# A state-space convolution with a routed low-rank layer on one core: odd x blocks turned by VectorE, outer-product tables made four heads at a time

## The reference, cut to what matters

```python
u_m = u * mask                                  # mask: position < length of the row
K[h, l] = 2 Re sum_n Cs[h, n] exp(dtA[h, n] l)  # 64 modes, 1024 taps
y = (causal convolution of u_m with K) + u_m * D ; y = y * mask
logits = y @ route_w.T                          # 8 experts
gate = one_hot(argmax) * max(logits)
out = x + sum_e gate[e] * (y @ A[e].T) @ Bw[e].T
```

## Time and profile before

| | us |
|---|---|
| three runs | 623.93, 623.76, 622.61; median 623.76 |
| the profiled execution, and its span | 623.93, 622.1 |
| PE, PEld (weight loads), DVE busy | 591.5, 530.9, 542.5 |
| ACT, POOL busy | 379.3, 372.9 |
| load of x, 512 KB, x64, median to landing | 4.1 |
| store, 512 KB, x63 | 4.8 |
| skewed load (Traw), 128 KB, x64 | 2.9 |

### The profile page before, as it was taken

How to read it: one execution, slowest core, us unless ns; L and a number is a source line. 1 busy time by engine, 2 the same in 40 slices (tenths; PEclk the granted TensorE clock), 3 DMA queues, 4 the chain that set the end, 5 groups by cost and what they waited for, 6 DMA issues and landing times.

```text
span 622.1 us, 13886 instructions
## 1 busy us (share of the span) xinstructions
PE 591.5 (95%) x3681; PEld 530.9 (85%) x3681; DVE 542.5 (87%) x1436; ACT 379.3 (61%) x1164; POOL 372.9 (60%) x474
## 2 busy tenths in 40 slices
PE   3379999999999999999999999999999999999995
PEld 2268998999899889988998998899899989988984
DVE  7778889988988898899889888988998898889874
ACT  3676656766676666567666766665676667666520
POOL 4465566557656755675576567556755765676520
PEclk9989999999999999999999999999999999999998
DMA  6023534453454345435534543454345345434521
GB/s 137 17 56 108 152 110 128 147 150 96 142 149 132 113 139 153 112 126 146 152 96 139 151 133 110 141 152 114 125 146 152 98 136 151 139 105 140 154 78 67
DMA packets 37074, 77.68 MB, mean 125 GB/s; under 512 B 11836, under 2 KB 20350, under 8 KB 36998
## 3 DMA queue, kind: packets, MB, share of 16 engines
q1 hardware_dynamic: 27846, 43.76, 29.5%
q10 hardware_dynamic: 9152, 33.03, 13.0%
HBM read 43.16 MB, written 33.62 MB: 123 GB/s over the span
## 4 chain that ended last, share of the span: by engine, by line
PE 92%; DVE 4%; issue 2%; POOL 1%; ACT 0%; DMA 0%; POOLq 0%
PE psYo L987 19%; PE psZ L1009 19%; PE psO L987 15%; PE psYe L987 12%; PE psS L987 11%; PE psO L1036 5%; PE psXe L1000 4%; PE psXo L1000 4%; PE psZ L1078 1%; PE psS L1047 1%; DMA logs<-in_L_cond_log_dt_dram 0%; DVE ex L693 0%; POOL Grev L436 0%; POOL wave L426 0%; DVE fraction L803 0%
## 5 line engine op out<-in xcount | busy, mean ns | idle before, releaser
L468 POOL TENSOR_TENSOR Slo<-Sf,Shi 128x384 fp32r<-128x384 f32 x64 | 64.9, 1015 | 210.1 <-ACT Shi L590 210.1
L852 DVE SCALAR_TENSOR_TENSOR brought<-Sf,tab,psS 64x128 f32<-64x128 f32 x256 | 89.0, 348 | 47.3 <-ACT Sf L585 40.9
L1009 PE MATMUL psZ<-Wt,Y 128*128 128x136 f32 x1024 | 129.6, 280 | 0.0
L1009 PEld LDWEIGHTS psZ<-Wt,Y 128*128 128x128 f32 x1024 | 127.8, 191 | 0.1
L531 ACT ACTIVATE Ghi<-Grev 128x256 fp32r<-128x256 f32 x64 | 26.8, 418 | 94.2 <-POOL Grev L436 94.2
L884 DVE TENSOR_TENSOR ost<-psO,xt 128x512 f32<-128x512 f32 x128 | 82.0, 676 | 2.2 <-PE psO L987 2.2
L461 POOL TENSOR_TENSOR Xlo<-xeven,Xhi 128x512 fp32r<-128x512 f32 x64 | 82.8, 1293 | 0.0
L568 ACT ACTIVATE Xhi<-psXe 128x512 fp32r<-128x512 f32 x64 | 38.2, 597 | 38.3 <-PE psXe L1000 38.3
L789 DVE TENSOR_SCALAR whole<-turns_t 128x256 f32<-128x256 f32 x64 | 57.8, 903 | 4.1 <-ACT turns_t L519 4.1
L585 ACT ACTIVATE Sf<-psS 128x128 f32<-128x128 f32 x64 | 17.7, 277 | 66.4 <-PE psS L987 66.4
L987 PE MATMUL psYo<-Xhi,Thi 128*128 128x512 f32 x128 | 55.6, 434 | 0.0
(11 more groups left out here) (194 smaller groups left out, 1670.8 us busy)
## 6 DMA issues: line engine op xcount, KB each, us to landing
xt<-in_x_dram SPq DMA_DIRECT2D x64, 512.0 KB, 4.1
out_dram<-ost ACTq DMA_DIRECT2D x63, 512.0 KB, 4.8
Traw<-kdram SPq DMA_DIRECT2D x64, 128.0 KB, 2.9
kdram<-krow SPq DMA_DIRECT2D x64, 1.0 KB
A_nat<-in_L_ffn_A_dram SPq DMA_DIRECT2D x1, 512.0 KB, 4.9
B_nat<-in_L_ffn_Bw_dram SPq DMA_DIRECT2D x8, 64.0 KB, 3.6
out_dram<-ost SPq DMA_DIRECT2D x2, 256.0 KB, 2.0
lens_i<-in_itok_B_dram SPq DMA_DIRECT2D x1, 64.0 KB, 3.6
```

The costliest lines, as they stand in the source:

```text
L468: pool.tensor_tensor(Slo[h.s2][:, :], Sf[h.s2][:, :], Shi[h.s2][:, :].bitcast(F32), ALU.subtract).then_inc(slo_done, 1)
L852: dve.scalar_tensor_tensor(brought[to, :], Sf[h.s2][fr, old], tab2[fr, BR, h.n:h.n + 1], psS[to, new], ALU.mult, ALU.add).then_inc(brought ...
L1009: last = pe.matmul(psZ[:, 0:NW], Y[:, j, c, :], Wt[:, 2 * c + j, :], start=(j == 0 and c == 0), stop=(j == 1 and c == NE - 1), skip_group_ ...
```

## The change

1. Odd x blocks. `turn_x` turns only the even blocks on PE. The odd ones are loaded a second time from DRAM, in 16 DMAs a head (32 rows by 4 groups by 32 positions, 128 bytes each), laid out so that a DVE transpose in 32x32 squares gives the position-major tile `xodd`. SP issues 11 of the 16, ACT 5. ACT rounds from `xodd`; the odd remainder goes to POOL (`x_lo_odd`).
2. `carry` writes what it brought into psS in place of the tile `brought`; the experts' `rank` is in psZ.
3. Tables. In place of 256 angles a head: 16 coarse and 16 fine ones, for four heads at once (`Part`), sines and magnitudes on those, and an outer product per head: real and imaginary halves (`mirror` makes the second set), a 512-wide product `both` and a sum of its halves.
4. The order in each engine's step, the start (steps for head 0 are written out, `run_steps` begins at 1) and the place of the exponentials of heads 8 to 63 (ACT, step 2) are different. The weight copies of the start go from DVE to ACT; the skewed load is issued at the start of SP's next step.

```diff
+        def load_blocks(eng, h, pieces):
+            need(eng, xodd_done, h.n - 1)
+            for g, c in pieces:
+                eng.dma_start(xblk[h.s2][g * G32:(g + 1) * G32, c, :, :],
+                              bass.AP(x.tensor, h.n * L + c * Q + P + g * G32,
+                                      [[H * L, G32], [G32 * H * L, G4], [1, G32]])
+                              ).then_inc(blk_in[h.s2], 16)
...
             def step(head):                                     # SP
+                if head(1).there and not is_head(head(0), 1):
+                    skew_kernel(head(1))
                 if head(2).there:
+                    load_blocks(sp, head(2), PIECES[:11])
                     load_x(head(2))
                     write_kernel(head(2))
-                    skew_kernel(head(2))
...
+            def weigh(part):                                    # POOL
+                for table, half, size in ((coarse, 0, COARSE), (fine, 0, FINE), (fine, 1, FINE)):
+                    pool.tensor_tensor(table[:, half, part.heads, :], wave[:, size, 0:part.n, :],
+                                       mag[:, size, part.heads, :], ALU.mult).then_inc(weighed, 1)
             def g_table(h):
+                pool.tensor_tensor(both[:, :, :, :],
+                    coarse[:, :, h.n, :].rearrange("p t (a b) -> p t a b", b=1).to_broadcast(wide),
+                    fine[:, :, h.n, :].rearrange("p t (a b) -> p t a b", a=1).to_broadcast(wide),
+                    ALU.mult).then_inc(both_done, 1)
+                pool.tensor_tensor(Grev[h.s2][:, :], both[:, 0, :, :].rearrange("p a b -> p (a b)"),
+                                   both[:, 1, :, :].rearrange("p a b -> p (a b)"), ALU.add).then_inc(grev_done, 1)
+            def x_lo_odd(h):
+                need(pool, xhi_odd, h.n + 1)
+                pool.tensor_tensor(Xlo[h.s2][:, 1, :], xodd[:, :], Xhi[h.s2][:, 1, :].bitcast(F32),
+                                   ALU.subtract).then_inc(xlo_odd, 1)
             def step(head):                                     # POOL
+                if part_at(head(8)): angle_steps(part_at(head(8)))
+                if part_at(head(6)): turn_parts(part_at(head(6)))
+                if part_at(head(4)): weigh(part_at(head(4)))
+                g_table(head(3)); x_lo_odd(head(1)); s_lo(head(0)); x_lo(head(1)); t_lo(head(1)); g_lo(head(3))
...
             def step(head):                                     # ACT
+                load_blocks(act, head(2), PIECES[11:])
+                store(head(-2)); first_state(head(0)); x_hi_odd(head(1)); m_matrix(head(3))
+                x_hi_even(head(1)); b_hi(head(2)); s_hi(head(0)); x_even(head(1)); t_hi(head(1)); g_hi(head(3))
+                if part_at(head(7)): turns(part_at(head(7)))    # four of 64 elements
+                if part_at(head(4)): mirror(part_at(head(4)))   # four half-height copies
+                w_hi(head(-1)); k_row(head(2))
+                if is_head(head(0), 2): magnitudes(slice(2 * FIRST, H))
+                if part_at(head(5)): sines(part_at(head(5)))
...
+            def turn_blocks(h):                                 # DVE
+                need(dve, blk_in[h.s2], (h.half + 1) * 16 * G4 * NE)
+                need(dve, xlo_odd, h.n)
+                dve.transpose(xodd[:, :], xblk[h.s2][:, :, :, :].rearrange("p c g i -> p (c g i)")
+                              ).then_inc(xodd_done, 1)
...
-                        dve.scalar_tensor_tensor(brought[to, :], Sf[h.s2][fr, old],
+                        dve.scalar_tensor_tensor(psS[to, new], Sf[h.s2][fr, old],
...
             def step(head):                                     # DVE
+                turn_blocks(head(1)); carry(head(0)); largest(head(-1)); first_largest(head(-1))
+                first_best(head(-1)); gates(head(-1)); gated(head(-1)); b_lo(head(2)); w_lo(head(-1))
+                cut(head(0), 0); cut(head(0), 1); add(head(-1), 0); add(head(-1), 1)
+                if part_at(head(7)): whole_turns(part_at(head(7)))
+                if part_at(head(6)): fractions(part_at(head(6))); clamp(part_at(head(6)))
...
             def step(head):                                     # PE
+                bring(head(0)); turn_x(head(1)); inputs(head(2)); project(head(-1)); within(head(0), 0)
+                within(head(0), 1); turn_k(head(2)); turn_wh(head(-1)); from_states(head(0)); up(head(-1), head(2))
```

More of the change, by code:

```diff
@@ L262, in __init__, with part_at @@
                 self.there = 0 <= n < H
+        class Part:
+            def __init__(self, k, start, stop):
+                self.k = k
+                self.start = start
+                self.n = stop - start
+                self.heads = slice(start, stop)
+        EDGES = list(range(0, H + 1, FIRST))
+        parts = [Part(k, EDGES[k], EDGES[k + 1]) for k in range(len(EDGES) - 1)]
+        def part_at(h):
+            for part in parts[2:]:
+                if part.start == h.n:
+                    return part
+            return None
         def is_head(h, *numbers):
@@ L409, in _, with angle_steps @@
             pool.wait_ge(tab_done, 1)
[L410 to L420, removed]
+            def angle_steps(part):
+                need(pool, turns_done, part.k * 4)
+                need(pool, frac2_done, part.k * 2)
+                for t, table in ((step_h, VH), (step_t, V), (step_l, VL)):
+                    pool.tensor_tensor(t[:, 0:part.n, :],
+                                       tab1[:, table, part.heads].rearrange("p (h a) -> p h a", a=1)
+                                       .to_broadcast([P, part.n, G16]),
+                                       grid16[:, :].rearrange("p (a g) -> p a g", a=1)
+                                       .to_broadcast([P, part.n, G16]), ALU.mult).then_inc(steps_done, 1)
@@ L471, in step @@
             def step(head):
-                if head(0).there and not is_head(head(0), 0):
+                if part_at(head(8)):
+                    angle_steps(part_at(head(8)))
+                if part_at(head(6)):
+                    turn_parts(part_at(head(6)))
+                if part_at(head(4)):
+                    weigh(part_at(head(4)))
+                if head(3).there and not is_head(head(0), 1):
+                    g_table(head(3))
+                if head(1).there:
+                    x_lo_odd(head(1))
+                if head(0).there:
                     s_lo(head(0))
@@ L475, in step @@
                     x_lo(head(1))
-                if head(3).there:
+                if head(3).there and is_head(head(0), 1):
                     g_table(head(3))
@@ new lines, in mirror @@
+            def mirror(part):
+                need(act, weighed, part.k * 3 + 3)
+                top, low = slice(0, N), slice(N, P)
+                for table, to, half, fr, scale in ((coarse, low, 1, top, 1.0), (coarse, top, 1, low, -1.0),
+                                                   (fine, low, 0, top, 1.0), (fine, top, 1, low, 1.0)):
+                    act.activation(table[to, half, part.heads, :], table[fr, half if table is fine else 0, part.heads, :],
+                                   ACT.Copy, scale=scale).then_inc(mirrored, 1)
@@ L904, in step @@
                     gated(head(-1))
-                if head(1).there and not is_head(head(0), 0):
-                    x_lo(head(1))
                 if head(2).there:
@@ L1123, in turn_tables @@
                 last.then_inc(tabs_turned, 1)
-            first = [Head(n) for n in range(2)]
-            pe.wait_ge(consts, 10)
-            turn_x(first[0], 0)
-            turn_x(first[0], 1)
+            first = [Head(n) for n in range(3)]
+            pe.wait_ge(consts, 9)
+            turn_x(first[0])
             pe.wait_ge(pack1_done, 1)
@@ L1153, in _ @@
                     last.then_inc(b_turned, 1)
+            inputs(first[0])
+            turn_k(first[0])
+            bring(first[0])
+            turn_x(first[1])
             inputs(first[1])
             turn_k(first[1])
-            pe.wait_ge(w_done, 3)
+            within(first[0], 0)
+            within(first[0], 1)
+            inputs(first[2])
+            from_states(first[0])
+            turn_k(first[2])
             run_steps(step)
```

448 lines of the change are left out of this document (246 added, 202 removed).

## The result

The changed kernel takes 679.7 us (median of 4 runs, 678.21 to 685.37) against 623.18 us before (4 runs, 622.46 to 623.93): a ratio of 1.0919, interval 1.0869 to 1.097. It is 9% slower; the forecast was 604.5 us, 590 to 627. The profiled execution of the changed kernel took 680.76 us.

A forecast was written before the change was run, and what follows sets the result against it. The prediction took PE to bound the kernel from the third step on; 623.93 us, less 26.4 for PE, plus 12 for the shared port, less 5 for the start, gave 604.5 us, range 590 to 627.

The forecast's parts named there:

- Issue: SP's queue: each small load holds it 0.32 us plus a 0.05 gap, a round of 6.0 of 8.56 us, no bound.
- The landing: SP's queue: from the k row's write to the skewed load, taken as 1.17 us of the round.
- Rival (d): SP and ACT queues: small loads at 0.6 us each hold SP 9.1 us a step; 625 us, chance 0.08.
- The pieces: DMA engines: 2048 pieces of 128 bytes a head at 15 ns, 1.9 us a step, hidden.
- (c): DMA engines become the bound: at 45 ns a piece 9.8 us a step, 667 us; chance 0.10.
- PE: Steady steps: four transposes a head go, 0.44 us, so the step falls from 9.00 to 8.56 us, -26.4 us in all.
- The cover: Steady step: the POOL state remainder ends 0.31 us before PE wants it, the slack read as next to run out.
- The transpose: DVE: the new 128x512 SBUF to SBUF transpose takes 0.65 us, between 0.64 and 1.3.
- (b): DVE: the transpose takes 1.3 us, waits for POOL and delays the carry; 634.5 us, chance 0.11.
- The shared port: DVE and POOL: a part's angle ops wait for POOL, 0.8 us for each of 15 parts, +12 us.
- The price of zero for the PSUM operands: DVE: the PSUM destinations of carry and rank cost nothing, within 0.05 us an op either way.
- The start: First steps: an earlier first `bring`, smaller angle sets and moved exponentials and weight copies gain 5 us.

The follow-up runs named there:

- e_xfirst: The changed kernel with the x load issued ahead of SP's eleven small loads instead of behind them: 625.18 us, 1.0042 of the kernel before.
- e_four_big: The changed kernel with each head's 2048 pieces, from other addresses of x, in four DMAs, two each on SP and ACT: 607.7 us.
- e_no_loads: The changed kernel without the small loads of heads 3 to 63, VectorE turning old data: 608.11 us, 0.9761 of the kernel before.
- e_ceiling: The kernel before the change with three of the four odd transposes of each head left out: 621.19 us, 0.9962 of the kernel before.
- e_quad: The changed kernel, complete, with the odd blocks of four heads in 16 DMAs of 512 pieces, four issued a step: 606.8 us.
- e_small: The changed kernel with its 16 small loads a head cut to 32 pieces each in place of 128: 662.92 us.
- e_inter: The changed kernel with SP's order changed to five small loads, skewed load, x load, six small loads, k row's write: 629.55 us.
- e_quad_sbuf: e_quad with the intermediate results of the carry and the ranks back in SBUF: 667.02 us, 1.0694 of the kernel before.

## Why the prediction was wrong, point by point

**Issue: the step that failed.** The prediction had SP's round at 1.17 + 13 x 0.37 = 6.0 us and "no bound under 0.57 us a piece". Both terms were too small. The 0.37 came from a 128-piece skewed load of the earlier trace rows; a small load takes about 0.5 and, over 62 rounds, 0.54: the mean step of 10.01 less 0.25 for the write, 2.67 for the wait behind it (165.3 / 62), 0.23 for ACT (14.5 / 62) and 0.93 for skew, x load and gaps leaves 5.9 us for eleven. The landing was the second term, read as a constant. It was 1.17 us in a kernel whose write went out long after the x load; now the write follows the 512 KB x load by 0.5 us, and write to skew is 2.9 us, 0.25 + 2.67. By these means neither error alone would have bound: 2.9 + 13 x 0.37 = 7.7 and 1.17 + 13 x 0.54 = 8.2 are both under 8.8; together they make 9.9. And 0.54 is still under the 0.57 that the prediction allowed for: what broke that margin is the landing. That the issue time alone would have been free is not shown, though: in e_xfirst, with a landing of 1.73 us on average, the round is 9.08 us and still binds. And the x load at the end of the round, said to have "most of a step" left, has none once the round is the step; e_xfirst, which moves only it, brings back 54.5 us, with its effect on the landing in them.

**Rival (d)** named the right mechanism and the right sign in the trace (SP without waits for ACT), but with the landing at 1.17 it came to 625 us, and it had a chance of 0.08.

**The pieces.** Right: hidden. e_four_big costs no time against e_no_loads, which rules out (c). The DMA share rises by 0.14 of a step of 8.81 us: 1.2 us, or 9.6 ns a piece, by an estimate, where I took 15. The Trainium skill, "DMA: Bandwidth & Descriptors", section "Specifications", asks for at least 512 B a transfer for line rate. No run here tests that rule: at 128 B and a share of 0.63 the engines are not full, and the time shows nothing of it.

**PE.** The 0.44 us are gone and a step of 8.56 us exists, but one in four. The cover that I read from the earlier trace rows, 0.31 us, was not the nearest: in e_ceiling, PE with 0.33 us less waits for DVE's `wh` after 0.04 us. That the saving comes through because the change moves `turn_wh` back too, which my sum put at nothing, is argued and not shown.

**The transpose.** 0.70 us for 0.65, and never long beside POOL, so (b) is out.

**The shared port.** Forecast 0.8 us a part; four steps of e_no_loads sum to 35.30 us, 1.06 over 4 x 8.56. The ops named are the ones lengthened (0.89 and 0.23 us in e_quad, up to 0.64 for the clamp beside `Grev` at 61.71 us of the changed kernel). Why the second and third step of four are long too (8.87, 8.69) was not followed op by op. The price of zero for the PSUM operands was right only as the difference to before; without them e_quad loses 60 us.

**The start.** Forecast -5. The second `bring` comes 5.7 us earlier (37.25 for 42.98 in e_no_loads), but the next step takes 13.7 us for 10.5, and at the fourth `bring` 2.6 us are left (59.93 for 62.52). The end, which I didn't price, gained 1.2: 18.6 us from the last `bring` to the end in e_no_loads for 19.7 (17.8 in the changed kernel).

**The account.** 679.7 - 604.5 = 75.2 us: the loads' issues, the landing and their clock 71.6, and by e_no_loads the start +2.4, the step +2.7 (60 x 0.045, 8.805 for the forecast mean of 8.76) and the end -1.2, which is 0.3 too much. Without the failed step the forecast would have been 3.6 us low; that this part came out so close is partly luck, since it priced the long steps at one in four and the second and third of four are long as well.

## What to carry to other kernels

Count a queue's round in DMAs, not in bytes, and add to it every wait that stands in it. A landing time read from the old trace holds only for the old order: ask what big load goes out just ahead. Where a saving needs many small loads, give each one as many pieces as its pattern can hold; and test how much the bounding engine can give back before the next one takes over.

## What the runs showed of the hardware

- The issue of a small load takes some 0.5 us of SP's queue with 32 pieces (eleven in 5.06 to 7.26 us, e_small) and with 128 (5.17 to 7.25, the changed kernel), and 0.48 with 512 in most steps, up to 1.2 in the others (e_quad). Right behind a 512 KB load it takes 0.62 on average, ahead of it 0.48 (e_inter); on ACT 0.44 (changed kernel). The skewed load takes 0.34 and the 1 KB write 0.25.
- 2048 pieces of 128 bytes a step, from rows 256 KB apart, cost no visible time at a DMA share of 0.63 (e_four_big).
- From the issue of a 1 KB write to that of the load that waits for its landing it is 1.2 us where the queue was idle before (the kernel before), 3.0 on average some 0.5 us behind a 512 KB load on the same queue (the changed kernel), and 1.73 behind eleven small loads with the 512 KB load ahead of them (e_xfirst).
- A DVE transpose of 128x512 float32 from SBUF to SBUF takes 0.70 to 0.71 us in all 64 steps of the changed kernel, though about half of them run beside a POOL op; ops of 0.35 us with two SBUF operands are lengthened, to 0.76 on average (e_quad_sbuf).
- PE's granted clock fell behind each of six waits of 2.03 to 2.84 us, to means of 0.57 to 0.69 over the next 4 us; the one priced cost 1.87 us. It did not fall behind a seventh of 2.06 us.
